# One block for the message and the node stage of a graph attention layer, with node work begun during the messages

## The reference

```python
h = jnp.maximum(_layernorm(x, axis=-1), 0.0)
Q, K, V = ((h @ W).reshape(n, H, HD) for W in (Wq, Wk, Wv))
scores = jnp.einsum('ehd,ehd->eh', Q[dst], K[src]) * SCALE
attn_max = jnp.zeros((n, H)).at[dst].max(scores)
w = jnp.exp(scores - attn_max[dst])
attn_sum = jnp.zeros((n, H)).at[dst].add(w)
w = w / (attn_sum[dst] + 1e-08)
out = jnp.zeros((n, H, HD)).at[dst].add(V[src] * w[:, :, None])
out = out.reshape(n, 256) @ Wo_w + Wo_b
out = _layernorm(h + out, ln1_g, ln1_b)
ffn = gelu(out @ ffn_w1 + ffn_b1) @ ffn_w2 + ffn_b2      # exact gelu
return x + _layernorm(out + ffn, ln2_g, ln2_b)
```

## Time and profile before

| | |
|---|---|
| median of 3 runs | 1828.78 us (1828.08 to 1831.19) |
| the profiled execution | 1828.51 us, its span 1826.8 us |
| mean granted TensorE clock | 0.955 of full speed |
| busy share of PE, DVE, ACT, POOL | 90%, 83%, 70%, 71% |
| score stage | about 0 to 314 us |
| softmax stage | to 362 us |
| message stage | to 534 us |
| node stage | to 1826.8 us |
| DMA traffic | 309.48 MB, mean 169 GB/s |

### The profile page before, as it was taken

One profiled execution on the slowest core, in us unless ns is written; L12 is line 12 of the kernel. 1 busy time (PEld: TensorE's weight loads), 2 busy tenths in 40 slices (PEclk: granted clock), 3 DMA queues, 4 the chain that ended last, 5 costly groups with the idle time before them and its releaser, 6 DMA issues.

```text
span 1826.8 us, 31063 instructions
## 1 busy us (share of the span) xinstructions
PE 1650.9 (90%) x10411; PEld 1441.2 (79%) x10411; DVE 1515.3 (83%) x4604; ACT 1280.9 (70%) x2366; POOL 1295.5 (71%) x1313
## 2 busy tenths in 40 slices
PE   4899997299803999999999999999999999999997
PEld 4888887167702888888888888888888888888886
DVE  3888885677503899999999999999999999999986
ACT  3777775022203888888888888888888888888884
POOL 7777640057734777878878778778778778788783
PEclk8999999589955999999999999999999999999999
DMA  5899895034326677767777777777777677677761
GB/s 161 263 299 303 292 267 196 26 101 135 113 86 167 135 165 171 170 167 166 173 168 162 176 171 162 171 174 164 167 171 170 165 169 170 167 165 173 169 129 57
DMA packets 133619, 309.48 MB, mean 169 GB/s; under 512 B 14622, under 2 KB 69614, under 8 KB 133460
## 3 DMA queue, kind: packets, MB, share of 16 engines
q0 software_dynamic: 42624, 139.33, 37.8%
q1 hardware_dynamic: 90836, 168.17, 27.6%
HBM read 140.66 MB, written 118.20 MB: 142 GB/s over the span
## 4 chain that ended last, share of the span: by engine, by line
PE 67%; DMA 1%; DVE 1%; POOL 1%; ACT 0%; SPq 0%; issue 0%; DVEq 0%; POOLq 0%; ACTq 0%
PE d_F L1031 31%; PE d_Y L1042 31%; PE d_T L1018 6%; DMA d_fb_row<-in_fb 1%; PE d_Y L1008 0%; DMA d_z<-agg_scratch 0%; ACT d_zn L943 0%; PE d_F L1001 0%; SPq L767 0%; POOL d_zx_rstd L828 0%; POOL d_u L815 0%; POOL d_u L813 0%; ACT d_z L954 0%; DVE d_y_stats L887 0%; DVE d_zx_stats L900 0%
## 5 line engine op out<-in xcount | busy, mean ns | idle before, releaser
L1042 PE MATMUL d_Y<-d_w_hi,d_act_hi 128*128 128x256 f32 x1568 | 458.1, 292 | 0.0
L1042 PE MATMUL d_Y<-d_w_lo,d_act_hi 128*128 128x256 f32 x1568 | 441.5, 282 | 0.0
L1042 PE MATMUL d_Y<-d_w_hi,d_act_lo 128*128 128x256 f32 x1568 | 441.1, 281 | 0.0
L943 ACT ACTIVATE d_zn<-d_z,d_zx_nmr,d_zx_rstd 128x256 f32<-128x256 f32 x392 | 224.2, 596 | 151.1 <-POOL d_zx_nmr L831 151.1
L1031 PE MATMUL d_F<-d_zt_hi,d_w_hi 128*128 128x512 f32 x784 | 321.1, 410 | 2.0 <-DVE d_zt_lo L863 1.4
L1031 PE MATMUL d_F<-d_zt_hi,d_w_lo 128*128 128x512 f32 x784 | 310.1, 396 | 0.0
L1031 PE MATMUL d_F<-d_zt_lo,d_w_hi 128*128 128x512 f32 x784 | 310.0, 395 | 0.0
L963 ACT ACTIVATE d_F<-d_F,d_fb_col 128x512 f32<-128x512 f32 x392 | 259.5, 662 | 59.2 <-PE d_F L1031 59.0
L813 POOL TENSOR_TENSOR d_u<-d_zn,d_g_row 128x1024 f32<-128x1024 f32 x98 | 293.8, 2998 | 6.0 <-ACT d_zn L943 6.0
L1042 PEld LDWEIGHTS d_Y<-d_w_hi,d_act_lo 128*128 128x128 f32 x1568 | 296.0, 189 | 0.0
L1042 PEld LDWEIGHTS d_Y<-d_w_hi,d_act_hi 128*128 128x128 f32 x1568 | 295.7, 189 | 0.0
(11 more groups left out here) (163 smaller groups left out, 3728.2 us busy)
## 6 DMA issues: line engine op xcount, KB each, us to landing
agg_scratch<-a_bias_row SPq DMA_DIRECT2D x50, 1024.0 KB
d_x<-in_x SPq DMA_DIRECT2D x98, 512.0 KB, 4.2
d_z<-agg_scratch POOLq DMA_DIRECT2D x98, 512.0 KB, 5.6
d_x<-d_b_wide POOLq DMA_DIRECT2D x98, 512.0 KB, 7.5
out<-d_o SPq DMA_DIRECT2D x98, 512.0 KB, 2.9
c_cont<-cont_scratch SPq DMA_DIRECT2D x25, 256.0 KB, 3.4
a_xd<-in_x,a_idx POOLq DMA_INDIRECT x100
a_xs<-in_x,a_idx POOLq DMA_INDIRECT x100
```

Source lines behind the costliest of these rows:

```text
L943: ins = nc.scalar.activation(zn[gz % 2][:, j, :], z[gz % ZR][:, j, :], ACT.Identity, bias=zx_nmr[:, at % NR, 0, j:j + 1], scale=zx_rstd[:, ...
L1042: ins = nc.tensor.matmul(Y[s % 2][:, j, :], a[:, c, j * P:(j + 1) * P], w[:, c, :], start=False, stop=(c == KF - 1 and w is w2_lo), skip_g ...
```

## The change

In `score_stage`, for steps s from 1 on, DVE does the low parts of side 0 ahead of the head sums. `message_stage` and `node_stage` become one function with one block: each engine's node instructions follow its message instructions without a meeting of the engines, and POOL waits on the scatters' own semaphores. To make room, the node tiles x, z, zn, u, o, b2_wide, w1_raw and w2_raw are laid in vt, where the messages have already read it, and T, FF share the banks of A.

During the messages, SP loads the seven short vectors ahead of the first alpha and cont, the weights at step 4, six x tiles at steps 5 to 13, and b2_wide at step 16. DVE splits the weights in steps 6 to 11 and takes the statistics of the first four x tiles in steps 13 to 16, with a root that uses ACT's Sqrt; ACT does their Relu norms behind groups 19 to 22 and loads the Gelu table after its last group. The eight matmuls that opened Y are gone, and 48 matmuls without use (HEAT) stand ahead of PE's first transposes. In the node loop FIRST is -3 in place of -6, groups 0 to 3 of x are left out of the loop's x work (`late`), and b2 is added to x one step later.

```diff
@@ score_stage, vector @@
                         products(s)
+                        low_part(s + 1, 0)
                         head_sums(s)
-                        low_part(s + 1, 0)
                         inverse_root(s + 2)
@@ message_node_stage @@
+        low_banks = ctx.enter_context(nc.psum_tensor("low_banks", [P, 4, GR], f32))
+        A = [low_banks[:, 2 * r:2 * r + 2, :] for r in range(2)]
+        T, FF = low_banks[:, 0, :], low_banks[:, 1:4, :]
+        XE = 4
+        X_FREE = (5, 6, 7, 9, 11, 13)
+        flat = vt[:].rearrange("p k e -> p (k e)")
+        xt = [rows_at(13 + r) for r in range(XR)]
+        z = [rows_at(3 + r) for r in range(ZR)]
-        FIRST, LAST = -6, NG + 1
+        FIRST, LAST = -3, NG + 1
+        HEAT = 48
+        def late(g):
+            return XE <= g < NG
@@ sync @@
                 for to, of in vectors:
                     sp.dma_start(to[:], of).then_inc(w_in, 16)
+                for c in range(-3, EG):
+                    step(Step(c))
+                    if c == 4:
+                        sp.wait_ge(msg_done, KD * 4)
+                        sp.dma_start(w1_raw, w1.rearrange("(k p) n -> p k n", p=P)).then_inc(w_in, 16)
+                        sp.dma_start(w2_raw, w2.rearrange("(k p) n -> p k n", p=P)).then_inc(w_in, 16)
+                    if c in X_FREE:
+                        g = X_FREE.index(c)
+                        sp.wait_ge(msg_done, KD * c)
+                        sp.dma_start(xt[g], rows_of(x, g)).then_inc(x_in[g], 16)
+                    if c == 16:
+                        sp.wait_ge(msg_done, KD * 16)
+                        sp.dma_start(b2_wide, b2_of).then_inc(b2_row_in, 16)
@@ tensor, after the messages @@
-                for r in range(2):
-                    for j in range(0, GT, 2):
-                        ins = nc.tensor.matmul(Y[r][:, j:j + 2, :], ident[:], w2_raw[:, j:j + 2, :], start=True, stop=True)
-                ins.then_inc(y_open, 1)
+                for n in range(HEAT):
+                    nc.tensor.matmul(FF[:, 2, :], w1_hi[:, 0, 0:P], w1_hi[:, n % KD, :], start=True, stop=True)
@@ vector, the message loop @@
+                for c in range(0, EG):
+                    step(Step(c))
+                    if 6 <= c < 12:
+                        weights(c - 6)
+                    if 13 <= c < 13 + XE:
+                        early_statistics(c - 13)
+                    if c == 13 + XE:
+                        dve.wait_ge(emv_done, XE * GT)
+                        nc.vector.tensor_scalar(e_veps[:], e_mv[:, :, :, 1], LN_EPS, None, ALU.add).then_inc(e_veps_done, 1)
+                    if c == 13 + XE + 1:
+                        early_root()
@@ scalar, in the message loop and after it @@
+                    if g == 13 + XE:
+                        act.wait_ge(e_veps_done, 1)
+                        nc.scalar.activation(e_std[:], e_veps[:], ACT.Sqrt).then_inc(e_std_done, 1)
+                    if 13 + XE + 2 <= g < 13 + 2 * XE + 2:
+                        early = g - 13 - XE - 2
+                        act.wait_ge(e_root, 5)
+                        for j in range(GT):
+                            ins = nc.scalar.activation(z[early][:, j, :], xt[early][:, j, :], ACT.Relu,
+                                                       bias=e_nmr[:, early, j:j + 1], scale=e_rstd[:, early, j:j + 1])
+                        ins.then_inc(h_done, 1)
+                nc.scalar.activation(gelu_ready[:], e_rstd[:, 0, 0:1], ACT.Gelu)
+                act.wait_ge(prep_d, PREP)
@@ gpsimd, between the scatters and the node loop, and in it @@
                 for r in range(4):
                     pool.wait_ge(scattered[r], 16 * GT * ((EG + 3 - r) // 4))
+                pool.wait_ge(prep_d, PREP)
+                pool.wait_ge(b2_row_in, 16)
...
+                    g = s + 2
+                    if there(g):
+                        pool.dma_start(xt[g % XR], b2_wide, accum_op=ALU.add).then_inc(b2_in[g % XR], 16)
```

More of the change, by code:

```diff
@@ new lines, in message_node_stage, with sb_first @@
+        zx_stats, zx_mv = sb("d_zx_stats", [P, NR, 2, GT, 6]), sb("d_zx_mv", [P, NR, 2, GT, 2])
+        zx_nmean, zx_veps = sb("d_zx_nmean", [P, NR, 2, GT]), sb("d_zx_veps", [P, NR, 2, GT])
+        zx_rstd, zx_nmr = sb("d_zx_rstd", [P, NR, 2, GT]), sb("d_zx_nmr", [P, NR, 2, GT])
+        y_stats, y_mv = sb("d_y_stats", [P, 2, GT, 6]), sb("d_y_mv", [P, 2, GT, 2])
+        y_veps, y_rstd = sb("d_y_veps", [P, 2, GT]), sb("d_y_rstd", [P, 2, GT])
+        with ExitStack() as first:
+            def sb_first(name, shape, dt=f32):
+                return first.enter_context(nc.sbuf_tensor(name, shape, dt))
+            msg = [sb_first(f"c_msg{r}", [P, KD, GR]) for r in range(2)]
+            total = [sb_first(f"c_total{r}", [P, KD, GR]) for r in range(2)]
+            rows = [sb_first(f"c_rows{r}", [P, GT, D]) for r in range(4)]
@@ L553, in message_stage, with there, wide, rows_of @@
+        HEAT = 48
+        def there(g):
+            return 0 <= g < NG
+        def late(g):
+            return XE <= g < NG
+        def wide(row):
+            return row[:].rearrange("p (j d) -> p j d", j=1).broadcast_to([P, GT, D])
+        def rows_of(table, g):
+            at = g * GR if g < NG - 1 else N - GR
+            return table[bass.ds(at, GR), :].rearrange("(p j) d -> p j d", j=GT)
         with nc.Block() as block:
@@ L569, in step @@
                           .then_inc(group_in[r], 16)
-                for c in range(FIRST, EG):
+                for to, of in vectors:
+                    sp.dma_start(to[:], of).then_inc(w_in, 16)
+                for c in range(-3, EG):
                     step(Step(c))
+                    if c == 4:
[9 more added lines that the diff above has]
+                        sp.dma_start(b2_wide, b2_of).then_inc(b2_row_in, 16)
+                for s in range(FIRST, LAST):
+                    g = s + 6
+                    if there(g) and g >= len(X_FREE):
+                        if g >= XR:
+                            sp.wait_ge(o_done, g + 1 - XR)
+                        else:
+                            sp.wait_ge(msg_done, KD * EG)
+                        sp.dma_start(xt[g % XR], rows_of(x, g)).then_inc(x_in[g % XR], 16)
+                    g = s - 1
+                    if there(g):
+                        sp.wait_ge(o_done, g + 1)
+                        if g == NG - 1:
+                            sp.wait_ge(stored[(g - 1) % 2], 16 * ((g - 1) // 2 + 1))
+                        sp.dma_start(rows_of(out, g), o[g % 2]).then_inc(stored[g % 2], 16)
+                for r in range(2):
+                    sp.wait_ge(stored[r], 16 * ((NG + 1 - r) // 2))
             @block.tensor
@@ L598, in step @@
                             for k in range(KD):
[L599 removed]
+                                ins = nc.tensor.matmul(Y[r][:, j, :], total[r][:, k, j * P:(j + 1) * P], wo_rows[:, k, :],
                                                        start=False, stop=(k == KD - 1), skip_group_check=True)
                         ins.then_inc(y_done, 1)
[L602 removed]
+                for c in range(-3, EG):
```

714 lines of the change are left out of this document (342 added, 372 removed).

## The result

The changed kernel took 1773.58 us (median of 4 runs, 1771.84 to 1774.66) beside 1828.48 for the kernel before: ratio 0.9696, interval 0.9679 to 0.9713. The forecast was 1780.7 with a range of 1768 to 1794. On another occasion the same pair gave 1772.94 beside 1829.72, ratio 0.9692 (0.9679 to 0.9705). The profiled span fell from 1826.8 to 1771.5, and the 55.3 us divide as follows. T is again the moment at which the last scatter has left POOL, and a row that falls is negative.

What follows compares the result with a forecast made beforehand. PE matmuls bound the node stage, PE and its low-part wait the score step, POOL's scatters the message stage's end; -7.9 + 5.0 + 2.0 - 46.35 - 0.6 = -47.85 from 1828.51 gives 1780.7 us, range 1768 to 1794.

Steps and rivals of the forecast that it cites:

- Head sums behind the low parts: Score stage: low parts start 1.03 us earlier, PE gains 0.31 in each of 22 steps; 7.9 us saved in all.
- Rival 2: Score stage does not follow, because fills and gathers or the head sums' new place take PE's 0.31: 1788.6 us; 7%.
- Start of the messages: Message stage start: seven vector loads ahead of the first alpha and cont delay the first scatter and T by 5.0 us.
- Scatters: Message stage: DVE's added work meets scatters more often, giving 2 more long ones: +2.0 us, bounds -6 and +11.
- Rival 4: Message stage: DVE's added work and shifted phase make most short scatters long: 1856 us, slower from 53 more on; 3%.
- Early work at nothing: Message stage: node work and loads placed between messages fit free ACT, DVE and DMA time, costing nothing.
- The seam: Message to node stage: first FFN matmul at T + 17.8 in place of T + 64.15, 46.35 us saved.
- Rival 1: Seam: POOL needs the 8.6 us pause after its scatters in any case, so it remains: 1789.3 us; 12%.
- No gain from the warm-up: Seam: PE idles after the 48 warm-up matmuls, so the first FFN is as cold as before; no gain or loss.
- Rival 3: Seam: warm-up works, PE still at 2.4 GHz at T + 12.8, first step and transposes faster: about 1777 us; 7%.
- The Gelu table: First node step: table load moves ahead of T, half its 1.28 us counted: 0.6 us saved, bounds 0 and 1.3.
- Node steps unchanged: Node stage: the 97 further steps of 12.53 us and the tail stay as before, 0 us.

Runs made afterwards that it cites:

- fills_behind: Changed kernel with the 50 agg_scratch fills issued behind the score steps instead of two per step: 1927.04 us, ratio 1.0534; with head sums first again, 1937.70 us.
- vectors_behind: Changed kernel with SP's seven vector loads moved behind the first four alpha and cont loads: 1903.85 us, ratio 0.9754 to the kernel before.
- work_behind: Changed kernel with DVE's early node work and ACT's Relu groups moved behind the last message, loads still early: 1903.06 us, ratio 0.9747.
- first two sets: Eight follow-up runs, each set on its own chip, in which the kernel before took 1953.7 and 1952.9 us.
- order_only: Kernel before with only the low parts of side 0 put ahead of the head sums: 1952.27 us, ratio 1.000.

## Why the prediction was right, point by point

- **Head sums behind the low parts: right mechanism, size too small.** I wrote "it gains all of its 0.31 in 22 steps". The step fell by 0.53 to 0.535 (fills_behind against its old order, and the two first profiles), 13.2 us over the stage in place of 7.9. Read from PE's transposes of side 1, the 22 steps gave 11.7 in place of my 6.9, the first one 1.1 for my 1.03, and 0.5 lay ahead of the first of them. The step of mine that failed was to take the shown idle time for the stall: 0.16 us of it lay under the modelled end of the last matmul, and I had the rows for it (0.40 long, 0.24 apart). Rival 2, that DMA at 0.92 would hold the step, is refuted.
- **Start of the messages: right, 5.8 for 5.0,** and vectors_behind gave it back. The path was right, the nearness of the size in part luck: b_wide's excess of 5.1 stood for a later landing, and the landing gave 1.24. The issue gave 3.34, as my bound of 3.3 had it, and 1.3 lay on the way to the first rows.
- **Scatters: 2.7 for 2.0, for a reason that the runs do not bear out.** With the work taken from between the messages as many were long (work_behind), so that the number came near is luck; what made them more than 15 stays open. Rival 4 named the same reason, and 25 long ones were the most in any run, where it needed 53 more.
- **Early work at nothing: right.** POOL had no wait in the middle of the messages in the changed kernel.
- **The seam: right, 46.1 for 46.35,** with each part near its place: 1.42 and 5.25 for 1.2 and 5.61, the norm at T + 10.85 for 10.6, and 7.18 from there to the FFN for 7.2. Rival 1 is refuted by POOL's 1.42.
- **No gain from the warm-up: right.** The 48 matmuls ended at T - 5.8, and the clock was at 0.50 from 520, T + 0.1. Rival 3 is refuted twice: the clock does not hold, not even over the 2.82 us of work_behind, and where PE was warm at its transposes the first gelu still waited for POOL's root.
- **The Gelu table: 1.1 for 0.6 in the first profile, not settled.** G was 15.31 to 15.35 in the three profiles with the old seam and 13.64 to 14.98 in the eleven of the changed form, so it fell each time, by 0.3 to 1.7; but that spread is more than the term, and no run moved the table load alone.
- **Node steps unchanged: wrong.** I wrote "the 97 further steps of the node stage and the tail are as before". They fell by 0.037 each, 3.5 us in 96. The prediction named this as what could make it wrong ("0.1 us in it is worth 10") and had no row for it, since I had looked at the order of the work and not at where the tiles move.

Together: 47.85 expected, 55.3 measured, inside the range but by two terms that I had too small or at nothing; 5.3 of the difference comes from the score stage, 3.5 from the node steps and 0.5 from the first group, less 1.8 from the softmax, the start and the scatters.

## What to carry to other kernels

Where an engine's ends are modelled, read a stall from start to start: the interval across the wait less the interval between its neighbours, not the idle time shown. When a rewrite moves tiles, its effect on the loop that reads them is a term of its own, to be had by moving the tiles alone. Work without use that keeps an engine warm must be tied to the event that it bridges; a fixed count cost 12 us when its start moved, and before adding it, see whether another engine sets the end of that stretch anyway.

## What was not expected of the hardware

**PE can stand still with nothing to wait for,** that is, with nothing that the profile shows. In the first two sets it did so in almost each score step up to POOL's last gather. PE's timeline in order_only, in the middle of the products for Q:

```profile
137.09 0.28 PE L348 MATMUL a_Q<-a_wq_hi,a_htd_lo 128*128 128x256 f32 x1
137.57 0.37 PE L348 MATMUL a_Q<-a_wq_hi,a_htd_hi 128*128 128x256 f32 x1 [0.21 <-issue]
138.99 0.28 PE L348 MATMUL a_Q<-a_wq_lo,a_htd_hi 128*128 128x256 f32 x1 [1.04 <-issue]
139.70 0.38 PE L348 MATMUL a_Q<-a_wq_hi,a_htd_lo 128*128 128x256 f32 x1 [0.43 <-issue]
```

These matmuls of one row need no further operand, and follow each other at 0.48, 1.42 and 0.71 us instead of 0.12. Then ACT, DVE and POOL's gathers fall behind in turn, the next products run at 0.21 us each, and the step takes 15.5 in place of 10.9. In all, the score stage of order_only had 25 spacings of over 0.6 us inside one row of products (23.1 us), the kernel before in its own profile none. There was one long stall more, ahead of the first group's transposes of side 1:

```profile
50.50 1.94 PE L368 MATMUL a_T<-a_ident,a_hs 128*128 128x128 f32 x8 [24.54 <-issue]
```

ACT (22.55 us) and DVE (27.24) stood still over the same stretch, while POOL went on issuing gathers. And in the middle of the messages PE stood five times for 0.81 to 1.57 us between 577 and 584, until POOL had no rows:

```profile
587.32 1.62 POOL L682 DMA_INDIRECT agg_scratch<-c_rows,c_row_of  x1 [5.20 <-ACT c_rows L657]
```

Without the usual 0.3 of issue these are 4.9 us; with 4.5 us of longer scatters they make up the 9.5 us by which M is above that of the kernel before. In all eight profiles of the first two sets the score steps are steady from the last gather on (column E), although the fills go on, so the stalls there went together with the gathers. They went with the occasion (or the chip) and not with the kernel, DMA was less busy than otherwise (0.64), and no run here shows their cause.

**SBUF addresses alone were worth 1.4% of a 128x256 float32r matmul** (0.1224 to 0.1207 us from start to start), 0.04 us of a step of 12.5, at equal order and clock. The two profiles with the old addresses have 0.1223 and 0.1224, the twelve with the new ones 0.1207 to 0.1209.
